# Two tiles' variances raised to a power in one GpSimd instruction, with the normalisation and the write one tile later

## What is computed

```python
def _layernorm(x, axis=-1, eps=1e-05):
    m = jnp.mean(x, axis=axis, keepdims=True)
    v = jnp.var(x, axis=axis, keepdims=True)
    return (x - m) / jnp.sqrt(v + eps)
...
        gate_logits = jnp.einsum('bsd,ed->bse', x, gate_w) + gate_b + expert_bias
        top_idx = jnp.argmax(gate_logits, axis=-1)
        out = jnp.zeros_like(x)
        for e in range(NUM_EXPERTS):
            mask = (top_idx == e)[..., None].astype(x.dtype)
            h = jax.nn.relu(jnp.einsum('bsd,df->bsf', x, w1[e]) + b1[e])
            y = jnp.einsum('bsf,fd->bsd', h, w2[e]) + b2[e]
            out = out + mask * y
...
    x = _layernorm(x + _L0_attn_ref(x, L0_attn_W_DQ, L0_attn_W_UQ, L0_attn_W_QR, L0_attn_W_DKV, L0_attn_W_UK, L0_attn_W_UV, L0_attn_W_KR, L0_attn_W_O), axis=-1)
    x = _layernorm(x + _L0_ffn_ref(x, L0_ffn_gate_w, L0_ffn_gate_b, L0_ffn_expert_bias, L0_ffn_w1, L0_ffn_b1, L0_ffn_w2, L0_ffn_b2), axis=-1)
```

## Time and profile before

| | us |
|---|---|
| median of 3 runs | 440.21 (438.69 to 440.54) |
| the profiled execution, its own time | 439.83 |
| its span, first to last instruction | 438.1 |
| the expert stage within it | about 341 to 438.1 |
| PE busy in the span | 416.3 (95%) |
| POOL busy in the span | 152.1 (35%) |

### The profile page before, as it was taken

One profiled execution on the slowest core, in us unless ns is written; L12 is line 12 of the kernel. 1 busy time (PEld: TensorE's weight loads), 2 busy tenths in 40 slices (PEclk: granted clock), 3 DMA queues, 4 the chain that ended last, 5 costly groups with the idle time before them and its releaser, 6 DMA issues. The chain is left out here.

```text
span 438.1 us, 12324 instructions
## 1 busy us (share of the span) xinstructions
PE 416.3 (95%) x4235; PEld 230.2 (53%) x4235; DVE 362.1 (83%) x824; ACT 356.4 (81%) x568; POOL 152.1 (35%) x164
## 2 busy tenths in 40 slices
PE   8899999999999999999999999998999899699993
PEld 6533344444443444444444444443444698599992
DVE  3978897999998889999987999999878578377764
ACT  3979999999998999998899999998889564376661
POOL 8221001315213013512401314212001466688887
PEclk9889999999999999999999999999899999899998
DMA  5268510668671135544500760674410255477640
GB/s 154 50 167 195 162 49 1 144 145 227 145 170 30 45 87 126 123 112 103 133 2 6 164 149 27 142 170 133 125 39 2 73 140 156 146 223 197 200 136 20
DMA packets 33005, 50.62 MB, mean 116 GB/s; under 512 B 5627, under 2 KB 16545, under 8 KB 32944
## 3 DMA queue, kind: packets, MB, share of 16 engines
q1 hardware_dynamic: 25488, 36.51, 34.1%
q10 hardware_dynamic: 5184, 9.05, 7.3%
q0 software_dynamic: 2272, 4.27, 2.9%
HBM read 21.35 MB, written 5.33 MB: 61 GB/s over the span
## 5 line engine op out<-in xcount | busy, mean ns | idle before, releaser
L1032 ACT ACTIVATE prob<-ring 128x1024 f32<-128x1024 f32 x288 | 274.5, 1039 | 25.8 <-PE ring L1224 25.0
L1242 PE MATMUL o_acc<-prob,v_stat 128*32 128x512 f32 (+3 forms) x1536 | 155.8, 501 | 2.9 <-DVE prob L705 2.1
L1224 PE MATMUL ring<-queries,keys 32*128 32x512 f32 (+3 forms) x1536 | 126.8, 385 | 0.4 <-DVE queries L665 0.4
L1224 PEld LDWEIGHTS ring<-queries,keys 32*128 32x128 f32 x1536 | 71.0, 187 | 71.4 <-issue 48.0
L691 DVE TENSOR_SCALAR prob<-prob 128x2048 f32<-128x2048 f32 x64 | 77.4, 1220 | 7.2 <-ACT prob L1032 6.8
L705 DVE SCALAR_TENSOR_TENSOR prob<-prob,mask_hi 128x1024 f32<-128x1024 f32 (+1 forms) x80 | 82.2, 1028 | 0.0
L1120 ACT ACTIVATE prob<-ring,b1T 128x128 f32<-128x128 f32 x156 | 44.6, 368 | 35.6 <-issue 16.4
L704 DVE TENSOR_SCALAR prob<-prob 128x1024 f32<-128x1024 f32 (+1 forms) x80 | 64.7, 808 | 6.6 <-ACT prob L1032 6.1
L584 POOL DMA_INDIRECT by_expert<-xrow,index x32 | 40.1, 1254 | 78.1 <-DVE index L800 71.0
L1242 PEld LDWEIGHTS o_acc<-prob,v_stat 128*32 128x32 f32 x1536 | 34.1, 109 | 57.2 <-issue 39.5
L565 POOL TENSOR_TENSOR rstd<-var_eps,const 128x4 f32<-128x4 f32 x8 | 16.4, 2048 | 92.0 <-DVE var_eps L748 92.0
(11 more groups left out here) (117 smaller groups left out, 343.5 us busy)
## 6 DMA issues: line engine op xcount, KB each, us to landing
queries<-query_parts SPq DMA_DIRECT2D x60, 256.0 KB, 4.0
v_stat<-in_w ACTq DMA_DIRECT2D x34, 256.0 KB
keys<-key_parts SPq DMA_DIRECT2D x60, 128.0 KB, 2.5
queries<-by_expert SPq DMA_DIRECT2D x39, 66.0 KB
xrow<-in_x_rows SPq DMA_DIRECT2D x8, 264.0 KB, 4.4
xT<-in_x_T SPq DMA_DIRECT2D x8, 256.0 KB, 3.0
v_stat<-in_w SPq DMA_DIRECT2D x5, 256.0 KB
out<-prob,queries POOLq DMA_INDIRECT x39
```

The lines of the kernel that those rows point to most:

```text
L1032: act.activation(prob[u % P_SLOTS][:, 2 * half:2 * half + 2, :].rearrange("p h s -> p (h s)"), slot(("score", u, half))[:], ACT.Exp, scale ...
L1224: last = pe.matmul(out[:, j % 2 * QC + off:j % 2 * QC + off + w], keys[hg][r, kt * P:(kt + 1) * P], queries[hg][r, qc, part, QC - w:QC], s ...
L1242: last = pe.matmul(o_acc[j * VW:(j + 1) * VW, QC - w:QC], v_stat[b % 2][:, hg, kt, j, :], prob[u % P_SLOTS][:, j, off:off + w], start=begi ...
```

## The change

GpSimd takes the variances of two tiles in one instruction, in every second step. `y_var` and `y_rstd` are two columns wide for that: tile c has column c % 2 of buffer c // 2 % 2. Since the power of an even tile now comes a step later, normalisation and write are both moved one step back (tile c - 3 in step c), the loops of DVE and POOL get one step more, and the rings of `x_b2`, `ys` and `y_mean` have five buffers in place of three. The 39th tile has a power of its own, one column wide.

```diff
-STAGES = 3
+STAGES = 5
...
-        y_var = [sb(f"y_var{i}", [P, 1]) for i in range(2)]
-        y_rstd = [sb(f"y_rstd{i}", [P, 1]) for i in range(2)]
+        y_var = [sb(f"y_var{i}", [P, 2]) for i in range(2)]
+        y_rstd = [sb(f"y_rstd{i}", [P, 2]) for i in range(2)]
...
             def y_inverse_std(c):
-                pool.wait_ge(y_vared, c + 1)
-                pool.tensor_tensor(y_rstd[c % 2][:], y_var[c % 2][:], const[:, CONST["half"]][:, 0:1],
+                w = min(2, TILES - c)
+                pool.wait_ge(y_vared, c + w)
+                pool.tensor_tensor(y_rstd[c // 2 % 2][:, 0:w], y_var[c // 2 % 2][:, 0:w], const[:, CONST["half"]][:, 0:w],
                                    ALU.pow).then_inc(y_rstd_ready, 1)
...
-            for c in range(TILES + 2):
-                if 1 <= c <= TILES:
-                    y_inverse_std(c - 1)
-                if c >= 2:
-                    write(c - 2)
+            for c in range(TILES + 3):
+                if 2 <= c <= TILES + 1 and c % 2 == 0:
+                    y_inverse_std(c - 2)
+                if c >= 3:
+                    write(c - 3)
                 if TAIL_AT.get(c) == "out":
                     inverse_std(LAST_HALF)
                 if c in ROUTE_AT:
...
-                dve.tensor_scalar(y_var[c % 2][:], y_mean[c % STAGES][:, 1:2], EPS, None, ALU.add).then_inc(y_vared, 1)
+                dve.tensor_scalar(y_var[c // 2 % 2][:, c % 2:c % 2 + 1], y_mean[c % STAGES][:, 1:2], EPS, None, ALU.add).then_inc(y_vared, 1)
 
             def y_norm(c):
-                dve.wait_ge(y_rstd_ready, c + 1)
+                dve.wait_ge(y_rstd_ready, c // 2 + 1)
...
-                dve.tensor_scalar(zs[c % RING][:], ys[c % STAGES][:], y_mean[c % STAGES][:, 0:1], y_rstd[c % 2][:],
+                dve.tensor_scalar(zs[c % RING][:], ys[c % STAGES][:], y_mean[c % STAGES][:, 0:1],
+                                  y_rstd[c // 2 % 2][:, c % 2:c % 2 + 1],
                                   ALU.subtract, ALU.mult).then_inc(z_ready, 1)
...
-            for c in range(TILES + 2):
+            for c in range(TILES + 3):
                 if c < TILES:
                     residual(c)
                 if 1 <= c <= TILES:
...
                     y_statistics(c - 1)
-                if c >= 2:
-                    y_norm(c - 2)
+                if c >= 3:
+                    y_norm(c - 3)
                 if 1 <= c <= TILES:
                     y_moments(c - 1)
```

## The result

| | us |
|---|---|
| changed kernel, median of 15 runs | 443.94 (441.9 to 445.86) |
| kernel before, median of 15 runs beside them | 440.21 (437.2 to 443.79) |
| ratio, 95% interval | 1.0097, 1.0075 to 1.0119 |
| profiled execution of the changed kernel, its span | 443.85, 442.1 |

So it is about 1% slower, and beyond the upper end of the range that was forecast, 443.2. That is the first of six sessions. A session is a group of kernels that run one after another on one chip, with the kernel before run among them. The same changed kernel was run again in two more sessions and gave 1.0023 (0.9988 to 1.0057) and 1.0104 (1.0074 to 1.0134). The experiments came to be about that difference.

The account below looks back on a forecast made before the run. PE was taken to bound the steady stretch, POOL nearly full beside it. With 0 elsewhere, the end's 0.95 us gave 440.8 from the profiled 439.83, or 441.2 from the median; forecast 441.0 us, range 438.6 to 443.2.

Parts of the forecast that it names:

- In steps 17 to 38 that is worth nothing: PE sets the pace there: Steady stretch: saving 8 us of POOL's time gains nothing, as PE's period is 1.90 us a tile against POOL's 1.83.
- these two places: The two unsteady stretches, 370 to 390 us and from 430 us, said to be the only source of gain or loss.
- crowding: Around tile 12's ReLU: DMA issues of ACT and SP crowd; the change moves POOL's share about 1 us, adds none.
- The end: Last writes on POOL: write of tile 35 stands behind the pair's power, so the end comes 0.95 us later (0.79 to 1.27).
- The two-column power: POOL's power of two columns takes 0.74 us, between bounds of 0.58 and 1.06, in place of 1.16 for two singles.
- Steps 6 to 10: Write of tile 4 1.2 us later, last route 0.8 us earlier; taken as 0 in the sum.
- the rival of late loads: Last half sequence: load of tile 17 comes 2.2 us later, 1.1 beyond the slack, giving 443.2 us; chance 25%.
- The routes: Steps 9 and 10 on POOL: last route starts at 377.0 against 377.78, 4.5 us after tile 9's variance, not 5.3.
- The rival of a smaller crowded spell: Between 370 and 390 us: ACT's 3.31 us hold goes, PE gains about 2.1 us, giving 438.7 us; chance 15%.
- the forecast is wrong if a DVE normalisation waits for a power in the steady stretch: Sign against the forecast: DVE's normalisation held up by POOL's power in the steady stretch.
- POOL busy at 7.7 to 8 us in 10 from 400 us and PE still at 10.00: Sign for the forecast: from 400 us POOL's busy time falls from 8.69 us in 10 while PE stays full.
- the chance of 0.24 for slower: Whole kernel: chance of a time beyond the 0.5% border of 442.4 us; same had 0.68, faster 0.08.

Follow-up runs that it names:

- the delay alone: Kernel before with five buffers, normalisation and write a tile later, but single powers in each step: 441.24 us, ratio 1.0029; run again in session 6, 440.76 us, 1.0039.
- before again, session 3: Kernel before, no edit, run for a second profile: 440.16 us in one run.
- before again, session 5: Kernel before, no edit, run for a new profile: 439.1 us in the profiled run.
- changed again, session 5: Changed kernel, no edit, run again with a new profile: 439.73 us, ratio 1.0023.
- the one-column variant: Changed kernel with two one-column powers in a row in place of the two-column one: 448.09 us, ratio 1.0194; again in session 6, 446.68 us, 1.0166.

## Why the prediction was wrong

**The step that failed** is "In steps 17 to 38 that is worth nothing: PE sets the pace there". PE does set the pace, and POOL's lighter load was indeed worth nothing. The same goes for "A gain or a loss can only come from these two places". I summed POOL's work and did not ask what the new order does to the others: every second power between two writes is gone. In a session with held waits that costs 46.05 - 42.44 = 3.6 us in the first profile of each kernel (45.6 us in session 6, 3.1 more than the 42.5 of the delay alone beside it), the largest part of the 3.7 and 5.3 us between the medians in sessions 1 and 6. In session 5 the step is right: 42.4 us both. The trace of before had the warning. Its ReLU of tile 12 stood still for 3.31 us with nothing named, in a place where POOL's DMAs stand close behind each other. I called that crowding, noted that the change moves POOL's share and adds none there, and never asked where else the change makes POOL's DMAs stand close.

**The end** was right in its mechanism and a little small: 0.95 us forecast, with bounds of 0.79 and 1.27. Measured 6.5 - 5.3 = 1.2 us in session 1, the same with the delay alone, and 6.1 - 5.5 = 0.6 in session 5. The sum of session 5 with this term alone (0.6 of 439.5, 0.1%) lies within the interval of its 1.0023, which also takes in no change. The variance of tile 38 is ready at 435.33 + 0.15 = 435.48, and the last write starts 4.0 us after it (3.8 forecast, 2.8 before); in session 5 it is 434.92 - 431.15 = 3.8 us. The order is the one that was worked out, with its gaps of 0.19 and 0.30 us, and from the pair's power to the last write it took 5.44 us where 5.48 were forecast. What was taken too short is what comes before: POOL was still at the write of tile 34 (begun at 433.10), and the power began 0.36 us after the variance of tile 37 was ready (433.57 + 0.15), where 0.07 was forecast. In session 5 it was 0.09.

```profile
433.57 0.15 DVE L992 TENSOR_SCALAR y_var<-y_mean 128x1 f32<-128x1 f32 x1
...
435.33 0.15 DVE L992 TENSOR_SCALAR y_var<-y_mean 128x1 f32<-128x1 f32 x1
```

**The two-column power**: 0.74 us forecast, 0.742 in the mean with one one-column power among 20, 0.75 for single ones. An estimate by the Trainium skill's "GPSIMD Engine Reference", section 3.1, was 0.58; this trace does not agree. Its price fits an operation that costs little an element, and this power costs 161 ns a column.

**Steps 6 to 10**: 0 was forecast. SP's six writes of zero rows, then the loads from tile 17, in the changed kernel:

```profile
366.18 9.16 SPq L397 DMA_DIRECT2D by_expert<-pad_row  x6
379.26 7.24 SPq L529 DMA_DIRECT2D queries<-by_expert  x6
```

The load of tile 17 is issued at 379.26, earlier than the 381.10 of the earlier trace rows, but the whole expert stage began 3.1 us earlier in this profile. Counted from the first product of tile 0:

| profile | write of tile 4 | load of tile 16 | load of tile 17 | first product of tile 17 |
|---|---|---|---|---|
| before, session 1 | 21.2 | 25.8 | 39.2 | 45.8 |
| changed, session 1 | 22.8 | 26.4 | 40.4 | 48.2 |
| before again, session 3 | 21.4 | 24.6 | 43.1 | 49.6 |
| before again, session 5 | 20.6 | 24.6 | 39.9 | 46.4 |
| changed again, session 5 | 21.6 | 25.2 | 39.3 | 46.0 |

The write of tile 4 is 1.1 to 1.6 us later, as worked out (1.2). Whether the load of tile 17 and PE come later by it, as the rival of late loads has it, these profiles can't tell: in session 1 they do, in session 5 they don't, and the kernel before alone differs from itself by 3.8 us. The routes did not move as forecast: the last one was to start 4.5 us after the variance of tile 9 is ready, and started at 375.17, which is 5.3 us after 369.76 + 0.15, as before. I had taken the first pair of routes to end where the old order had them, 0.9 us after that variance; behind the write of tile 6, which began at 367.96, they ended 1.6 us after it.

```profile
367.96 1.06 POOL L615 DMA_INDIRECT out<-prob,queries  x1 [2.25 <-DVE prob L999]
...
370.59 0.96 POOL L585 DMA_INDIRECT by_expert<-xrow,index  x1 [0.30 <-issue]
...
375.17 0.96 POOL L585 DMA_INDIRECT by_expert<-xrow,index  x1 [0.30 <-issue]
```

The rival of a smaller crowded spell is not borne out: the ReLU of tile 13 was 5.6 us late in both kernels.

```profile
378.58 1.14 ACT L1125 ACTIVATE prob<-ring,b1T 128x128 f32<-128x128 f32 x4 [4.79 <-remote]
```

That rival erred in its price too (and the range gives its end as 438.6 where its own sum is 438.7, on which nothing hangs). Where the spell was gone, PE stood still all the same, now for the load of tile 17. The kernel before in session 5:

```profile
376.28 1.06 PE L1348 MATMUL ring<-prob,v_stat 128*128 128x128 f32 x8
382.20 0.47 PE L1338 MATMUL ring<-ident,queries 128*128 128x128 f32 x1 [4.87 <-DMA queries<-by_expert]
```

From tile 0 to tile 17 it took 46.4 us there, and 45.8 and 49.6 in the two profiles with the spell, so what the spell costs is not shown; the medians of the kernel before (439.0 to 440.2 us in all six sessions) hardly show it either.

**Of what would show it**, "the forecast is wrong if a DVE normalisation waits for a power in the steady stretch" named the wrong engine: DVE never did so in the changed kernel to any size (2.7 us of idle time ahead of all 39 normalisations, 2.5 of it the power's), ACT's waits did it. What did give the error away is "POOL busy at 7.7 to 8 us in 10 from 400 us and PE still at 10.00": neither came out. The forecast of 441.0 us is about what the one session without held waits in which the changed kernel ran comes to (1.0023 times 440.2 is 441.2); which kind of session it would be was not known beforehand, so that agreement is luck, and the chance of 0.24 for slower was too low for a place whose warning stood in the rows.

**Open**: what makes a session one kind or the other, and through what the DMAs of POOL reach ACT's wait. All profiles of a session that could show it were of one kind, but each kernel has only one in a session, so whether its other executions were of that kind too is not shown. Of the eleven of the changed kernel in session 6, three took 440.7 to 441.5 us and the others 443.2 to 446.0. No kernel that was tried beats the kernel before.

## What to carry to other kernels

When a change takes instructions away from an engine that issues DMAs, look at what they stood between: their length may have been the distance that another engine's waits needed. An idle share is not slack; compare the engine's period with that of the engine that sets the pace, for POOL had 0.07 us here where the idle share showed over 1 us in 10. And a loss that was seen in one session is not yet a property of the kernel: run both kernels again in another session before its cause is written down, and keep an unexplained idle time in the trace of before as a warning with a price.

## What the runs showed of the hardware that was not expected

**Held waits.** In four of six sessions ACT's wait for PE ended 1.6 to 1.8 us after POOL began a scattering DMA that followed another by 0.30 to 0.40 us, though PE had ended up to 1.5 us earlier; in two sessions ACT went on 0.13 to 0.23 us after PE with the same gaps. Longer chains of such DMAs go with longer holds: 4.8 to 5.9 us at tile 13, among a write, two routes, a write and two routes, except where powers stood between them (0.1 us) and in the one-column variant, where the longest hold fell on tile 14 (3.0 and 2.2 us). Idle time of ACT ahead of its ReLUs from 387 to 430 us, changed kernel of session 1 and of session 5:

```profile
L1125 ACT ACTIVATE prob<-ring,b1T 128x128 f32<-128x128 f32 x83 | 23.9, 370 | 16.3 <-PE ring L1353 8.4 <-issue 4.7 <-PE ring L1370 3.2
```

```profile
L1125 ACT ACTIVATE prob<-ring,b1T 128x128 f32<-128x128 f32 x88 | 25.1, 367 | 13.4 <-PE ring L1353 13.4
```

**SP's issues too.** The six writes of zero rows took 10.73 and 9.16 us on SP in session 1, and 7.4 to 10.8 us in all profiles with held waits but the one with powers between the routes (6.01); in the seven profiles without, 6.2 to 7.0. In session 5, the kernel before and the changed one:

```profile
366.13 6.75 SPq L396 DMA_DIRECT2D by_expert<-pad_row  x6
```

```profile
366.79 6.25 SPq L397 DMA_DIRECT2D by_expert<-pad_row  x6
```

The Trainium skill, in "DMA: Bandwidth & Descriptors", section on SWDGE, HWDGE and iDMA, says that DMAs issued from SP and ACT are untouched by one kind of interference, in which VectorE locks GpSimd out of the memory where it writes descriptors. That is another direction than the one seen here, where GpSimd's DMAs go with slow issues of SP; no run here tells whether the two have to do with each other.
